# A six-layer local-attention kernel on one core: projections, hidden and narrow products in 32-column tiles, scores and mixes in halves, another order of work, and the last group in a tail of its own

## The reference

```python
qkv = x @ Wqkv                      # 128 -> 3 x 1024, 16 heads of 64
q = l2norm(q) * qs; k = l2norm(k) * ksc
q = q * cos * scale + rotate_half(q) * sin * scale   # k alike, with 1 / scale
sim = einsum(q, k of this and the previous window of 32) * 8   # masked, softmax
x = x + (attn @ v) @ Wo
x = x + (a * gelu(gate)) @ W2 + b2  # after shift of half the features by one token, layer norm, W1: 128 -> 2 x 341
```

## Time and profile before

| | |
|---|---|
| median of 3 runs | 1618.8 us (1618.2 to 1619.11) |
| profiled execution, its own time | 1619.38 us |
| its span, first to last instruction | 1617.6 us |
| PE busy | 1544.3 us (95%) |
| PEld, DVE, ACT, POOL busy | 907.8, 1234.8, 1232.5, 1222.1 us (56, 76, 76, 76%) |
| mean granted clock of TensorE | 0.987 |

### The profile page before, as it was taken

How to read it: one execution, slowest core, us unless ns; L and a number is a source line. 1 busy time by engine, 2 the same in 40 slices (tenths; PEclk the granted TensorE clock), 3 DMA queues, 4 the chain that set the end, 5 groups by cost and what they waited for, 6 DMA issues and landing times.

```text
span 1617.6 us, 69676 instructions
## 1 busy us (share of the span) xinstructions
PE 1544.3 (95%) x30224; PEld 907.8 (56%) x30224; DVE 1234.8 (76%) x1693; ACT 1232.5 (76%) x2368; POOL 1222.1 (76%) x1051
## 2 busy tenths in 40 slices
PE   7879999999999999999999999999999999999995
PEld 6745556555555555555556555555565565555553
DVE  5488878778778778777877778778778788787873
ACT  4347787787787787887887887887887887887871
POOL 6169888777787778778777787787787787787861
PEclk9989999999999999999999999999999999999998
DMA  5000000100000100000100000100000000000000
GB/s 193 28 2 27 10 7 5 61 7 6 22 6 7 35 29 10 18 7 9 36 28 10 9 16 10 33 31 9 9 16 9 7 5 9 7 18 9 7 12 27
DMA packets 24545, 32.60 MB, mean 20 GB/s; under 512 B 2372, under 2 KB 21424, under 8 KB 23344
## 3 DMA queue, kind: packets, MB, share of 16 engines
q1 hardware_dynamic: 24240, 28.15, 5.4%
HBM read 20.80 MB, written 1.05 MB: 14 GB/s over the span
## 4 chain that ended last, share of the span: by engine, by line
PE 75%; ACT 7%; issue 5%; DVE 3%; POOL 1%; DMA 0%; ACTq 0%; SPq 0%; POOLq 0%; DVEq 0%
PE ring L274 20%; PE psq L254 18%; PE ring L262 9%; PE ring L308 8%; PE pss L292 7%; PE ring L325 4%; PE ring L318 4%; PE pss L283 2%; DVE qb L927 2%; ACT L1126 2%; ACT sq L1096 1%; ACT uT L1126 1%; ACT pr L1100 1%; ACT kT L1107 1%; PE ring L649 1%
## 5 line engine op out<-in xcount | busy, mean ns | idle before, releaser
L254 PE MATMUL psq<-wqk,x0S 128*128 128x512 f32 x768 | 379.4, 617 | 4.0 <-issue 3.1
L274 PE MATMUL ring<-mh,x0S 128*32 128x512 f32 x3072 | 369.6, 598 | 7.4 <-ACT uT L1126 7.4
L1305 POOL TENSOR_TENSOR qa<-qa,qb 128x1024 f32<-128x1024 f32 x96 | 228.9, 2384 | 63.0 <-DVE qb L848 62.9
L1361 POOL TENSOR_TENSOR pr<-pr,rden 128x1024 f32<-128x1024 f32 x96 | 183.9, 1915 | 88.3 <-DVE rden L824 88.0
L1357 POOL TENSOR_TENSOR qa<-qa,qb 128x1024 f32<-128x1024 f32 x96 | 226.7, 2361 | 0.4 <-DVE qb L927 0.3
L254 PEld LDWEIGHTS psq<-wqk,x0S 128*128 128x128 f32 x768 | 135.8, 192 | 130.0 <-issue 120.8
L308 PEld LDWEIGHTS ring<-u,pT 128*32 128x32 f32 x6144 | 172.9, 111 | 61.4 <-issue 61.4
L904 DVE TENSOR_TENSOR qa<-psq,tab 128x1024 f32<-128x1024 f32 x96 | 117.5, 1224 | 105.5 <-PE psq L254 105.5
L308 PE MATMUL ring<-u,pT 128*32 128x128 f32 x6144 | 187.0, 274 | 3.2 <-ACT pT L1228 3.2
L1323 POOL TENSOR_TENSOR qa<-qa,rn 128x1024 f32<-128x1024 f32 x96 | 182.7, 1903 | 7.5
L274 PEld LDWEIGHTS ring<-mh,x0S 128*32 128x32 f32 x3072 | 80.0, 109 | 190.5 <-issue 172.6
(11 more groups left out here) (174 smaller groups left out, 2819.8 us busy)
## 6 DMA issues: line engine op xcount, KB each, us to landing
wqk<-in_wqk SPq DMA_DIRECT2D x6, 1024.0 KB, 4.9
mvT<-in_mvT SPq DMA_DIRECT2D x6, 512.0 KB, 5.6
wo<-in_wo SPq DMA_DIRECT2D x6, 512.0 KB, 8.7
xf<-x SPq DMA_DIRECT2D x24, 128.0 KB
xf<-x SPq DMA_DIRECT2D x24, 127.0 KB
rope<-in_rope SPq DMA_DIRECT2D x1, 2048.0 KB, 10.0
w<-in_w SPq DMA_DIRECT2D x6, 341.0 KB, 3.8
xmid<-in_x SPq DMA_DIRECT2D x4, 256.0 KB, 4.0
```

What stands on the lines that cost most here:

```text
L254: return mm(psq[:, 512 * (n % 2):512 * (n % 2) + 512], x0S[:, tile * P:tile * P + P], wqk[:, l % 2, 512 * n:512 * n + 512], start=True, st ...
L274: last = mm(bank[WIN * g:WIN * g + WIN, :], x0S[:, tile * P + WIN * w:tile * P + WIN * w + WIN], mh[:, l % 2, g, :, :].rearrange("p j n -> ...
L1305: g_.tensor_tensor(qa[:, t % 2, 0:1024], qa[:, t % 2, 0:1024], qb[:, 0:1024], ALU.add).then_inc(sum_q, 1)
L1361: g_.tensor_tensor(p4[t % 2], p4[t % 2], rden[:, :].unsqueeze(1).unsqueeze(3).broadcast_to([P, 2, HEADS, WIN]), ALU.mult).then_inc(p_ready, 1)
```

## The change

**TensorE's shapes.** `project`, `hidden` and `narrow` are no longer one product over 128 columns of the array each, but four (three for the third hidden block) over 32 columns each, with the same rows moving through: the same arithmetic and the same output. `scores` and `mix` are cut into two halves that stand at two places of a step.

```diff
-                return mm(psq[:, 512 * (n % 2):512 * (n % 2) + 512], x0S[:, tile * P:tile * P + P],
-                          wqk[:, l % 2, 512 * n:512 * n + 512], start=True, stop=True)
+                for w in range(NWIN):
+                    last = mm(psq[WIN * w:WIN * w + WIN, 512 * (n % 2):512 * (n % 2) + 512],
+                              x0S[:, tile * P + WIN * w:tile * P + WIN * w + WIN],
+                              wqk[:, l % 2, 512 * n:512 * n + 512], start=True, stop=True)
+                return last
...
-            def scores(t):
+            def scores(t, half):
-                for pair in range(PAIRS):
+                for pair in range(4 * half, 4 * half + 4):
...
-            def mix(bank, t):
+            def mix(bank, t, part):
-                for b in range(4):
+                for b in (2 * part, 2 * part + 1):
...
-                return mm(bank[0:n, :], w1[:, col:col + n], xnT[:, :], start=True, stop=True)
+                for c in range(0, n, WIN):
+                    m = min(WIN, n - c)
+                    last = mm(bank[c:c + m, :], w1[:, col + c:col + c + m], xnT[:, :], start=True, stop=True)
+                return last
...
-                        last = mm(bank[:, k * P:k * P + P], uT[0:n, j, k * P:k * P + P], w2[0:n, j, :],
-                                  start=(j == 0), stop=(j == 2))
+                        for w in range(NWIN):
+                            rows = slice(WIN * w, WIN * w + WIN)
+                            last = mm(bank[rows, k * P:k * P + P], uT[0:n, j, k * P + WIN * w:k * P + WIN * w + WIN],
+                                      w2[0:n, j, :], start=(j == 0), stop=(j == 2))
```

```diff
+TAIL = [(0, 3), (3, 1)]
+DONE = STEPS + 7
...
+            def late_rows(v):
+                k0, n = TAIL[v]
+                bank, m = take("TL", v)
+                ybank, use = place["Y", STEPS - QUAD + k0 + n - 1]
+                pe.wait_ge(freed[ybank], use + 1)
...
+                for d in range(2):
+                    tiles = slice(1 + TILES - QUAD + k0 - d, 1 + TILES - QUAD + k0 - d + n)
+                    last = mm(ring[bank][:, 0:n * HD], late[:, d * P:d * P + P], x1[:, 1, tiles, :].rearrange("p k n -> p (k n)"),
+                              start=(d == 0), stop=(d == 1))
...
+            late_rows(0)
+            late_rows(1)
+            for s in range(DONE, STEPS + 19):
+                step(s)
+            for v in range(len(TAIL)):
+                tail_turn(v)
+                for k in range(3):
+                    tail_hidden(v, k, 1)
+                    tail_hidden(v, k, 0)
+                if v > 0:
+                    tail_narrow(v - 1)
+            tail_narrow(len(TAIL) - 1)
...
+            for v in range(len(TAIL)):
+                tail_hat(v)
+            tail_turned(0)
+            for v in range(len(TAIL)):
+                if v > 0:
+                    tail_turned(v)
+                for k in range(3):
+                    tail_gelu(v, k)
```

More of the change, by code:

```diff
@@ L498, in _, with step @@
             features(0)
-            for s in range(STEPS + 17):
-                t = s - 7
+            def step(s):
+                t = s - 6
                 if 0 <= t < STEPS:
-                    bank, n = take("U2", t)
-                    wait(pe, freed[bank], n)
-                    values(ring[bank], t, 2).then_inc(filled[bank], 1)
                     bank, n = take("U3", t)
@@ new lines, in tail_turn, with tail_hidden @@
+            def tail_turn(v):
+                k0, n = TAIL[v]
+                bank, m = take("TF", v)
+                pe.wait_ge(t_xh, v + 1)
+                wait(pe, freed[bank], m)
+                for k in range(n):
+                    last = tr(ring[bank][:, k * P:k * P + P], xh[:, (k0 + k) * P:(k0 + k) * P + P], ident[:, :])
+                last.then_inc(filled[bank], 1)
+            def tail_hidden(v, k, gate):
+                k0, n = TAIL[v]
+                bank, m = take(("TA%d", "TG%d")[gate] % k, v)
+                nbank, use = place["TF", v]
+                pe.wait_ge(freed[nbank], use + 1)
+                wait(pe, freed[bank], m)
+                h0, rows = HBLK[k]
+                col = h0 + gate * HID
+                mm(ring[bank][0:rows, 0:n * P], w1[:, col:col + rows], xnT[:, k0 * P:(k0 + n) * P],
+                   start=True, stop=True).then_inc(filled[bank], 1)
@@ new lines, in tail_narrow @@
+            def tail_narrow(v):
+                k0, n = TAIL[v]
+                bank, m = take("TZ", v)
+                for k in range(3):
+                    abank, use = place["TA%d" % k, v]
+                    pe.wait_ge(freed[abank], use + 1)
+                wait(pe, freed[bank], m)
+                for k in range(n):
+                    for j, (h0, rows) in enumerate(HBLK):
+                        rows += j == 2
+                        last = mm(ring[bank][:, k * P:k * P + P], uT[0:rows, j, (k0 + k) * P:(k0 + k) * P + P], w2[0:rows, j, :],
+                                  start=(j == 0), stop=(j == 2))
+                last.then_inc(filled[bank], 1)
@@ new lines, in _, with tail_stats @@
+            for s in range(DONE):
+                step(s)
+            def tail_stats(u):
+                k0, n = TAIL[u]
+                bank, m = place["TL", u]
+                dve.wait_ge(freed[bank], m + 1)
+                for k in range(k0, k0 + n):
+                    last = v.bn_stats(bst[:, k, :], xf[:, :, k, :])
+                last.then_inc(t_bst, 1)
+                dve.wait_ge(t_bst, u + 1)
+                for k in range(k0, k0 + n):
+                    last = v.bn_aggr(mv[:, k, :], bst[:, k, :])
+                last.then_inc(t_mv, 1)
@@ L1202, in _ @@
[L1202 to L1210 removed]
+                i = group_at(s, 11)
@@ new lines, in _ @@
+            for s in range(DONE):
+                step(s)
+            for v, (k0, n) in enumerate(TAIL):
+                tiles = slice(1 + TILES - QUAD + k0, 1 + TILES - QUAD + k0 + n)
+                bank, m = place["TL", v]
+                act.wait_ge(filled[bank], m + 1)
+                cp(xf[:, 0, k0:k0 + n, :], x1[:, 0, tiles, :])
+                cp(xf[:, 1, k0:k0 + n, :], ring[bank][:, 0:n * HD].rearrange("p (k n) -> p k n", n=HD)).then_inc(freed[bank], 1)
+            for s in range(DONE, STEPS + 19):
+                step(s)
```

871 lines of the change are left out of this document (494 added, 377 removed).

## The result

| | before | after |
|---|---|---|
| median | 1618.95 us (1618.2 to 1619.3, 4 runs) | 1578.48 us (1575.09 to 1580.13, 4 runs) |
| profiled execution, its span | 1619.38, 1617.6 us | 1580.13, 1578.3 us |

The ratio is 0.9748, 95% interval 0.9731 to 0.9765: the change makes the kernel 2.5% faster. Against the forecast of 1584.1 the median is 5.6 us lower, inside the range.

The account below looks back on a forecast made before the run. In the loop only TensorE's own time counts, at the two ends latencies do. Terms -32.6 + 9.6 - 5.3 - 3 + 3 - 4.0 - 2.4 = -34.7 us, applied to 1618.8, give 1584.1 us; range 1566 to 1606.

Parts of the forecast that it names:

- The loop: TensorE's steps in the middle: base step -32.6 us, group parts +9.6, narrow products -5.3, waits -3.
- The base step: A loop step without group parts: six shape changes instead of eight, none entering full width; 0.34 us less, -32.6 in 96.
- F and X: Group parts now between scores and values: one shape change and one entry more each, 0.2 us; +8.6 us.
- Z: The narrow products: 2.64 us beside tiled work, 0.23 less, 23 times; -5.3 us.
- Waits: TensorE's waits for G1's Gelu shrink by 5 us, stalls grow by 2 with more matmuls; -3 us (+6 to -7).
- Filling: Start of the run: a tile's way is two steps longer, so more steps lack TensorE work; +3 us (-3 to +12).
- The end: Group 22's F and hidden products leave the time ahead of the last mix's end, -4.0 us; behind it -2.4 (+3 to -7).
- What has to stay hidden: Round trip between key projections through the other engines: 12.1 us against TensorE's lightest step of 12.6, hidden by half a microsecond.
- Four tiles on the same rows are slower: Rival: projection and hidden tiles reading the same rows stream slower; 0.11 us more a pass makes 1700 us; chance 0.05.
- The change of shape was not what was paid: Rival: the 0.095 us a border comes back at new borders, the loop gains only waits and Z; 1605 to 1612; chance 0.08.
- Another engine's round trip: Rival: semaphores and in-order queues lengthen the round trip, which then sets the light steps; 1605 to 1615 us; chance 0.13.
- More than that: Rival: lighter ACT and shorter bank queues also end waits no record shows as idle; 1550 to 1566 us; chance 0.09.

Follow-up runs that it names:

- e9: The kernel before with ACT's Gelu replaced by Square, which needs no table load of its own: 1611.17 us, ratio 0.9946.
- e11: The changed kernel with ACT's Gelu replaced by Square, which needs no table load of its own: 1576.67 us, ratio 0.9724 to the kernel before.
- e2: The changed kernel with projections, hidden and narrow products back in full width, so the new order alone: 1634.17 us, ratio 1.0081 to the kernel before.
- e6: The changed kernel with group 22's last-layer norm on DVE moved behind the tail's gate products of part 0: 1577.0 us, ratio 0.9738 to the kernel before.
- e7: The changed kernel with two dummy bf16 products behind each part of the learning rule's chain in steps 0 to 2: 1574.05 us, ratio 0.9715.
- e3: The changed kernel with the projection alone back in full width: 1621.66 us, ratio 1.0006 to the kernel before.
- e4: The changed kernel with the hidden products alone back in full width: 1594.74 us, ratio 0.984 to the kernel before.
- e5: The changed kernel with the scores in one piece at the place of their first half, behind the mask: 1634.92 us, ratio 1.0092 to the kernel before.
- e1: The kernel before with tiled projections, hidden and narrow products and nothing else, so shapes alone: 1614.76 us, ratio 0.9964.

## Why the prediction was right, term by term

The cause was right: TensorE's own time in the loop, by changes of shape. The sum was -34.7 us and the span gave -39.3. That it came so near owes something to luck: the loop gave 14 us more than its terms, filling and end 10 us less.

**The loop** was to give 32.6 - 9.6 + 5.3 + 3 = 31.3 us and gave about 45.6. Eight steps without an issue stall, before and after, show where:

```profile
L904 DVE TENSOR_TENSOR qa<-psq,tab x9: 1223/1224/1225, 1070.6 to 1192.8; 128x1024 f32<-128x1024 f32 x9
```

```profile
L940 DVE TENSOR_TENSOR qa<-psq,tab x9: 1206/1224/1225, 1030.9 to 1149.7; 128x1024 f32<-128x1024 f32 x9
```

122.2 and 118.8 us, so 1.7 us a group, 40.8 in 24. To take a group apart one needs a step of the kernel before that has neither F nor X:

```profile
169.24 0.71 PE L262 MATMUL ring<-ident,qa 64*128 64x64 f32 x16
...
179.51 0.72 PE L262 MATMUL ring<-ident,qa 64*128 64x64 f32 x16
180.34 1.98 PE L254 MATMUL psq<-wqk,x0S 128*128 128x512 f32 x4
182.26 0.71 PE L262 MATMUL ring<-ident,qa 64*128 64x64 f32 x16
```

It lasts 13.02 us, and 0.19 of them is a stop ahead of the projection (0.83 us behind the turn instead of 0.64), so 12.83.

- *The base step* was to save 0.34 us and saves 0.37: 12.83 before, 12.46 after. -35.5 us instead of -32.6. The two projections lasted 1.92 and 1.91 between turns and last 1.83 each. The scores cost 0.18 more in two halves. The prediction counts 0.095 of it among its borders, so the "I take 0.05" for the cold start of the second half was too little and 0.085 is what it came to.
- *F and X* were to cost 0.2 more each than before. They last 0.52 and 0.49 before and 0.59 and 0.58 now, but before they also spared the projection beside them a border or an entry (1.82 and 1.81 instead of 1.92 and 1.91). So they cost 0.43 and 0.40 then, and 0.16 and 0.19 more now: +7 instead of +8.6. A merge takes 1.09 us as before, nothing instead of +1.0.
- *Hidden products* were "nothing". A group without a stall takes 60.16 us in e9, whose TensorE has the same work as before, and 58.83 after (1399.33 to 1458.16). Less four base steps, F, X and Z, the twelve passes are 5.1 us before and 5.2 after: nothing, as predicted.
- *Z* saves 0.12 itself (2.75 start to start, 2.87 before) and 0.12 as a neighbour, since the query projection ahead of it has no exit: 0.24, as worked out.
- *Waits.* The waits for the Gelu of G1 are gone. They lasted 0.39 us each start to start (1.03 from the turn to the values, at 969.20, instead of 0.64), 9 us in 23, where the records say 7.4 and the prediction took 5. By e9 and e11 the table loads cost 9.7 us before and 2 to 4 after.

Together these make -42, and TensorE's own time in them 1.33 us a group, 32 in 24 where the prediction had 28. The other 4 us fit the issue stalls, which fell from 8.5 to 2.1 us in 1000 where I had them grow by 2. So the step of the loop that was mis-sized is the one on waits: -3 in the sum, some -13 measured.

**Filling** was +3. To the first key pass it is +6.6, of which some 2.5 belong to this one execution: the pass starts at 89.9 us here, at 86.9 to 87.7 in e2 to e6 and e11, at 83.3 before. TensorE is idle 22.8 of 84 us between 76 and 160, 14.7 before: 8 us more, under the 10 that I had named as a sign of error, but at a clock of 0.76 instead of 0.85. I had counted idle time and not the clock that goes with it. e7 shows what it costs: 4 us. This is the step of the filling that failed.

**The end** was to give 4.0 ahead of the last mix and 2.4 behind it. The first can't be read by itself; with 45.6 from the loop, +6.6 at the start and nothing behind the mix, 0.3 us are left for it together with the later part of the filling. Behind the mix it is 34.9 us as before. The tail's turn was worked out at 14.3 us and stands at 14.66 (1558.06), and what comes behind it is too short in the prediction: the products of 384 columns, at 0.68 each, have a stop in them of 1.31 us while DVE normalizes group 22 (the part that e6 moves), and the last tile's turn and six products take 2.57 us instead of 1.6. Ahead of the turn, Z ran at a lower clock, 4.49 us instead of the 2.84 of other executions. In e3, e4 and e5, which have the same tail and Z at 2.84, it is 33.0 to 33.3 us. So the tail gives 1.6 to 1.9 where its Z runs at the full clock, against 2.4 forecast.

**What has to stay hidden** held. TensorE waits for ACT's squares of the keys 8.0 us in all, 5.4 of them between 76 and 160 us, and not between 442 and 1442. But I had DVE's first key pass wait for TensorE in every step; of 67 steps in the middle it does so in 26, in 26 it waits for the rotary table that POOL makes, and in 15 for nothing:

```profile
L940 DVE TENSOR_TENSOR qa<-psq,tab x67: 1203/1224/1225, 449.2 to 1433.0; 128x1024 f32<-128x1024 f32 x67
its engine sat idle before it (us, times) until:
  POOL tab L1532: 59.5, 26
  PE ring L275: 37.3, 26
```

In the kernel before it was TensorE in 64 of 65. So POOL now holds DVE's key pass as often as TensorE does, which the prediction didn't see. How little slack is left e5 shows: it takes 0.79 us from between the turn and the query projection and 0.58 come back as waits, so some 0.2 us of it was slack. The prediction's half microsecond was for the whole round.

**Rivals.** *Four tiles on the same rows are slower*: refuted. Four passes take 1.71 us start to start with tiled work behind (945.39 to 947.10 ahead of a Z), 0.43 each. The pass 1.26 times as long, which the prediction worked out from the 2.38 of the Trainium skill, TensorE: Matmul & The Clock Gate, Part 3, does not come about here; no run here timed three tiles by themselves. *The change of shape was not what was paid*: refuted by e2 to e4. *Another engine's round trip*: not here, but the next change meets it, by e5. *More than that*: a part of it came, in the waits. Of the signs, four steps in 59.7 us (four times 14.93, where the sign was 60.5), a turn of both halves at 1.14 and the end of the wait for Gelu came true; DVE waiting for TensorE in every step and an end of 32 to 33 us did not.

## What to carry to other kernels

A change of tile shape costs TensorE about 0.1 us at a border and another 0.1 on entering full width, and 0.03 us or nothing inside a run of one shape. So shapes and order must be planned together: here either alone gave 6 us or lost 14, both gave 40. When TensorE becomes faster, look at who sets when its banks are free: an ACT list with three table loads in a step kept that step at its old length. Before a block's cost is read from one row, look at what its neighbours last with and without it: X lasts 0.49 us in the kernel before and costs 0.40, since the projection behind it is spared an entry. And before two halves are joined to save TensorE 0.18 us, ask what the second one covers: here it was worth 56.

## What the runs showed that was not expected

- Dummy bf16 products of 512 columns, 0.22 us each, in places where TensorE waits anyway, raised the granted clock from 0.66 to 0.93 in the filling and gave 4 us.
- The clock of a short stretch behind a wait can differ from one execution to the next: Z(22) took 2.84 us in four profiles and 4.0 to 4.5 in three, behind the same wait of 2.0 us and without dummies in it. A change that seems to mend it needs more than one profile.
- Issue stalls of TensorE are not a matter of how many instructions there are: in 1000 us 12.2 with 35024 matmuls in e1, 2.1 with 34940 in the kernel after, 15.6 in e5 with the same 34940.
- A wait of TensorE is longer than its record: 0.24 us start to start where the record says 0.17, 0.34 where it says 0.15 or nothing. In e5 the records show 25 us of two waits that by estimate cost 56.
